# Mixer B of a hybrid Mamba/FFN kernel: a tile's diagonal products in two visits, and the second tile's other TensorE work in a new order

## What is computed

```python
proj = layernorm(x) @ in_proj_w * mup            # z (1024), xBC (1280), dt (64)
xBC = silu(causal_conv4(xBC) + conv_b)            # x, B, C
dt = softplus(dt + dt_bias);  A = -exp(A_log)
state = state * exp(dt * A) + (dt * x) outer B    # over time, here in chunks of 128 tokens
y = C . state + D * x
out = (y * rsqrt(mean(y**2) + eps)) * norm_w * silu(z)
return out @ out_proj_w
```

## Time and profile before

| | |
|---|---|
| median of 3 runs (lowest, highest) | 2864.6 us (2864.31, 2865.05) |
| span of the profiled execution | 2859.7 us |
| TensorE matmul busy | 2733.3 us, 96% |
| VectorE busy | 2009.9 us, 70% |
| ScalarE busy | 1527.0 us, 53% |
| GpSimd busy | 926.1 us, 32% |
| mean granted TensorE clock | 0.980 |

### The profile page before, as it was taken

One profiled execution on the slowest core, in us unless ns is written; L12 is line 12 of the kernel. 1 busy time (PEld: TensorE's weight loads), 2 busy tenths in 40 slices (PEclk: granted clock), 3 DMA queues, 4 the chain that ended last, 5 costly groups with the idle time before them and its releaser, 6 DMA issues. The chain is left out here.

```text
span 2859.7 us, 49906 instructions
## 1 busy us (share of the span) xinstructions
PE 2733.3 (96%) x17464; PEld 1845.0 (65%) x17464; DVE 2009.9 (70%) x3695; ACT 1527.0 (53%) x2418; POOL 926.1 (32%) x614
## 2 busy tenths in 40 slices
PE   7999999999999999996899999999999999997996
PEld 6777766777766665455666666666666666664453
DVE  5666666666666663377788888888888888885267
ACT  3444444445455442341577666766667776665242
POOL 2222223222223321232233444333333334332134
PEclk9999999999999999998999999999999999998998
DMA  4000000000000034145000000000000000022333
GB/s 125 23 23 22 22 22 22 23 28 29 22 22 22 16 121 152 45 147 204 12 23 22 22 22 16 21 22 22 15 15 22 22 22 22 15 95 89 112 118 133
DMA packets 79935, 139.59 MB, mean 49 GB/s; under 512 B 17896, under 2 KB 17896, under 8 KB 78832
## 3 DMA queue, kind: packets, MB, share of 16 engines
q1 hardware_dynamic: 70752, 125.92, 12.9%
q10 hardware_dynamic: 9104, 12.63, 1.4%
HBM read 104.98 MB, written 33.55 MB: 48 GB/s over the span
## 5 line engine op out<-in xcount | busy, mean ns | idle before, releaser
L655 PE MATMUL work<-b_xnT,shared_w 128*128 128x256 f32 x2304 | 545.8, 388 | 1.8 <-DVE b_parts L1192 1.3
L655 PE MATMUL work<-a_xnT,shared_w 128*128 128x256 f32 x2176 | 509.4, 392 | 1.3
L655 PEld LDWEIGHTS work<-b_xnT,shared_w 128*128 128x128 f32 x2304 | 426.1, 191 | 90.6 <-issue 30.1
L655 PEld LDWEIGHTS work<-a_xnT,shared_w 128*128 128x128 f32 x2176 | 419.0, 195 | 73.8 <-issue 12.3
L1232 DVE TENSOR_TENSOR b_decay<-b_decay,b_gt 128x1024 f32<-128x1024 f32 x256 | 351.7, 1395 | 119.3 <-ACT b_decay L943 115.8
L936 ACT ACTIVATE b_decay<-seg 128x1024 f32<-128x1024 f32 x256 | 248.5, 1029 | 112.0 <-PE seg L781 111.8
L943 ACT ACTIVATE b_decay<-b_decay 128x1024 f32<-128x1024 f32 x256 | 266.1, 1073 | 0.0
L1406 POOL TENSOR_TENSOR b_rhs<-b_l_side,of_head 128x1024 fp32r<-128x1024 f32 x32 | 82.0, 2563 | 552.4 <-DVE b_l_side L1201 552.4
L1441 POOL TENSOR_TENSOR a_y<-a_y,a_skip 128x1024 f32<-128x1024 f32 x32 | 90.9, 2840 | 484.1 <-DVE a_y L1221 484.1
L1111 DVE SCALAR_TENSOR_TENSOR shared_cv<-shared_pre,a_conv_w,shared_cv 128x256 f32<-128x256 f32 x432 | 189.7, 482 | 74.6 <-ACT shared_cv L880 68.9
L1111 DVE SCALAR_TENSOR_TENSOR shared_cv<-shared_pre,b_conv_w,shared_cv 128x256 f32<-128x256 f32 x480 | 232.1, 517 | 14.2 <-ACT shared_cv L880 6.3
(11 more groups left out here) (314 smaller groups left out, 4612.4 us busy)
## 6 DMA issues: line engine op xcount, KB each, us to landing
shared_x<-in_L_attn_a_x SPq DMA_DIRECT2D x16, 512.0 KB, 3.5
a_x_res<-in_L_attn_a_x SPq DMA_DIRECT2D x32, 256.0 KB, 2.6
x_mid<-a_x_res SPq DMA_DIRECT2D x32, 256.0 KB, 2.1
shared_w<-in_L_ffn_d_w SPq DMA_DIRECT2D x2, 4096.0 KB, 14.0
f_d_w<-in_L_ffn_d_w SPq DMA_DIRECT2D x2, 4096.0 KB, 14.5
f_x_res<-x_mid SPq DMA_DIRECT2D x8, 1024.0 KB, 5.9
f_bc_w<-x_mid SPq DMA_DIRECT2D x8, 1024.0 KB, 5.6
shared_x<-x_mid SPq DMA_DIRECT2D x16, 512.0 KB, 3.6
```

Source lines behind the costliest of these rows:

```text
L655: mm = nc.tensor.matmul(dst, w_in[:, k, col:col + m], xnT[:, k, :], start=(k == 0), stop=(k == KD - 1))
```

## The change

Only mixer B (NP > 1) is touched. The diagonal products of a tile are done in two visits of four slots. Unit 1 of the first tile moves ahead, between `pout` and `xnT1`. In the second tile `z1` and `z2` come right behind `rt0`, `sums` comes behind `state1`, and `out0` stands behind the last unit, ahead of the last visit. ScalarE's and VectorE's orders are rewritten to match: the multiplies of slots 4 to 7 of the second tile stand behind convolution pair (8, 9), the halo copy, the state add and the copy of the sums; the gate of the first tile comes in two halves at different places; the layer norm of the supertile after next moves from the second tile to the first.

```diff
@@ mixer_phase, the lists @@
-        if NP > 2:
-
-            fill1 = [[], [], [], ["z1"], [], ["z2"]] + [[]] * (NS - 6)
-
...
-                    + (["xnT0"] if nxt else []) + (["pout"] if prev else []) + (["xnT1"] if nxt else [])
+                    + (["xnT0"] if nxt else []) + (["pout"] if prev else [])
+                    + (["seg0.1"] if NP > 1 else []) + (["xnT1"] if nxt else [])
                     + ["ident0", "small1"])
...
+            if NP > 1:
+                def diagonal(j, half):
+                    return [f"ydiag{j}.{s}" for s in range(half * (NS // 2), (half + 1) * (NS // 2))]
+
+                def when(names):
+                    return names if nxt else []
+
+                steps += when(["dt"] + blocks[0:2]) + diagonal(0, 0)
+                steps += ["seg0.2"] + when(blocks[2:4]) + ["seg0.3"] + when(blocks[4:NB])
+                steps += state_steps(0) + diagonal(0, 1) + when(["z0a", "z0b"])
+                steps += ["rs0", "yoff1a", "yoff1b", "seg1.0", "rt0"] + when(["z1"])
+                steps += ["seg1.1"] + when(["z2"]) + ["ident1"] + diagonal(1, 0)
+                steps += ["seg1.2"] + state_steps(1) + when(["sums"]) + ["seg1.3", "out0"]
+                steps += when(["small0"]) + diagonal(1, 1)
+                return steps
@@ ScalarE's supertile (square and gate now take which halves) @@
+                    if NP > 1:
+                        slot_bound(sec, 0, 2)
                     if nxt:
                         xnT_copy(sec, 1)
+                    if NP > 1:
+                        slot_bound(sec, 0, 3)
+                        slot_exp(sec, 0, 2)
+                        slot_exp(sec, 0, 3)
+                        if nxt:
+                            softplus(sec)
+                            block_copy(sec, 0)
+                            block_copy(sec, 1)
+                        slot_bound(sec, 0, 4)
+                        slot_bound(sec, 0, 5)
+                        if nxt:
+                            block_copy(sec, 2)
+                        slot_exp(sec, 0, 4)
+                        if nxt:
+                            block_copy(sec, 3)
+                        slot_exp(sec, 0, 5)
+                        slot_bound(sec, 0, 6)
+                        if nxt:
+                            block_copy(sec, 4)
+                        slot_bound(sec, 0, 7)
+                        if nxt:
+                            block_copy(sec, 5)
+                        slot_exp(sec, 0, 6)
+                        if nxt:
+                            block_copy(sec, 6)
+                        slot_exp(sec, 0, 7)
+                        if nxt:
+                            block_copy(sec, 7)
+                            block_copy(sec, 8)
+                        square(2 * i, (0,))
+                        if nxt:
+                            block_copy(sec, 9)
+                        square(2 * i, (1,))
...
+                        for s in (0, 1):
+                            slot_bound(sec, 1, s)
+                        for s in (0, 1):
+                            slot_exp(sec, 1, s)
+                        out_rsqrt(2 * i)
+                        if nxt:
+                            z_copy(sec, "z1")
...
@@ VectorE's supertile @@
+                    if NP > 1 and sec.ln is not None:
+                        norm_stats(sec.ln)
                     small_sums(sec, 1)
                     if not prev:
                         norm_into_w_out()
+                    if NP > 1:
+                        slot_mult(sec, 0, 2)
+                        if nxt:
+                            dt_raw(sec)
+                        slot_mult(sec, 0, 3)
+                        if nxt:
+                            dt_finish(sec)
+                            conv_blocks(sec, (0, 1))
+                        gate(sec, 0, (0,))
+                        if sec.ln is not None:
+                            norm_apply(sec.ln)
+                        slot_mult(sec, 0, 4)
+                        if nxt:
+                            conv_blocks(sec, (2, 3))
+                        slot_mult(sec, 0, 5)
+                        if nxt:
+                            conv_blocks(sec, (4, 5))
+                        slot_mult(sec, 0, 6)
+                        slot_mult(sec, 0, 7)
+                        exponent_sides(2 * i + 1)
+                        state_add(sec, 0)
+                        gate(sec, 0, (1,))
+                        if nxt:
+                            conv_blocks(sec, (6, 7))
+                        square_sums(sec, "rs0")
+                        from_state(sec, 1)
+                        rms_var(sec, "rt0")
+                        slot_mult(sec, 1, 0)
+                        slot_mult(sec, 1, 1)
+                        if nxt:
+                            next_decays(sec)
+                            keep_column(sec)
+                        slot_mult(sec, 1, 2)
+                        slot_mult(sec, 1, 3)
+                        if nxt:
+                            conv_blocks(sec, (8, 9))
+                            halo(sec)
+                        state_add(sec, 1)
+                        if nxt:
+                            sums(sec)
+                        for s in (4, 5, 6, 7):
+                            slot_mult(sec, 1, s)
+                        out_scale(2 * i)
+                        out_add(sec, "out0", i, 0)
+                        if nxt:
+                            small_sums(sec, 0)
+                        gate(sec, 1)
+                        if nxt:
+                            exponent_sides(2 * sec.n)
+                        return
@@ GpSimd: norm_rsqrt now in tile_steps of the first tile @@
-                tile_steps(0, 0)
-                tile_steps(0, 1, ln=2)
+                tile_steps(0, 0, ln=2 if NP > 1 else None)
+                tile_steps(0, 1, ln=None if NP > 1 else 2)
```

35 lines of the change are left out of this document (28 added, 7 removed).

## The result

The changed kernel takes 2865.7 us (median of 20 runs, 2862.0 to 2872.8), the kernel before 2863.7 in the same comparison (20 runs): a ratio of **1.0013, 95% interval 1.0007 to 1.0019**. By the ratio it is 3.7 us slower, by the two medians 2.0; both are less than the 0.2% at which I had put the limit of a measurement. The profiled span is 2866.4 us (before 2859.7).

The account below looks back on a forecast made before the run. TensorE sets the period (78.18 of 78.63 us busy), fed by VectorE's chain. Fourteen supertiles +2.1, first +1.0, last +1.6 make +4.7 on the 2859.7 span, 2864.4; the median lies 4.9 above: 2869 us, range 2853 to 2883.

Parts of the forecast that it names:

- First tile -0.75: xT0 to the second tile's first unit: 0.70 and 0.20 saved, 0.15 lost by unit 1, so 50.85 us instead of 51.60.
- The chain to S + 15.40: Second tile, S its first unit's start: VectorE's multiplies, convolution pair, halo and state add let sums start at S + 15.40.
- Exclusion: VectorE instructions with two SBUF inputs and GpSimd's SBUF reads shut each other out, so multiply 2 works from S + 9.25.
- next_decays and keep_column follow (0.7): VectorE, second tile, from S + 7.37: these take 0.7 us unheld, so multiply 2 is issued at about S + 8.1.
- the over 2 us that I gave as a sign: Second tile on VectorE: multiply 2, held by GpSimd's decay of the state, should take over 2 us.
- TensorE's own way, 13.8 to sums and 12.53 behind: Second tile: TensorE's own work takes 13.8 us from S to sums, then 12.53 from sums through the next supertile's zza.
- Nothing for the first tile's waits, the loads and GpSimd's norm step: First tile's new waits, SyncE's later x load (about 13 us to spare) and GpSimd's power step are each priced at nothing.
- slower rival: First tile's blocks wait for ScalarE's copies: 0.75 us lost per supertile, 10.5 over fourteen, 2880 us; chance 0.2.
- Period +0.15: Per supertile, first tile -0.75 and second tile +0.90 give +0.15; +2.1 over fourteen, period 78.8 us.
- First supertile +1.0, last +1.6: First: statistics and a multiply ahead of dt, +1.0 (-1 to +3). Last: no fills, half visits stall ScalarE, +1.6 (0 to +5).
- Faster rival (the chain doesn't bind): VectorE's chain in the second tile doesn't bind: 2857 us with sharing, 2847 if it never binds; chance 0.2.
- The sharing reading: VectorE's multiply and GpSimd's decay run together instead of excluding each other: chain 0.85 us shorter, 12 over fourteen, 2857 us.

Follow-up runs that it names:

- first-tile-alone run: Against the kernel before, only each supertile's first tile has the new order, with the norm in it; second tile as before but for convolution pair (8, 9): 2846.4 us, 0.9941.
- run without the decay: Changed kernel with GpSimd's decay of the state in mixer B's second tile cut to one head, so the state is wrong: 2839.3 us (1 run).
- xw early in the kernel before: Kernel before, with GpSimd's two operations that make xw moved ahead of the sum into y1 in mixer B: 2898.2 us, 1.0119.
- second alone: Against the kernel before, only each supertile's second tile has the new order; the first tile and the norm's place stay as before: 2871.3 us, 1.0030.
- decays later: Changed kernel with next_decays and keep_column moved behind multiply 3 of the second tile on VectorE: 2865.9 us, 1.0012 to the kernel before.
- out0 early: Changed kernel with the second tile's output product moved right behind unit 2 and VectorE's order behind the halo copy changed to match: 2884.9 us, 1.0089 to the kernel before.
- the same move of xw: GpSimd's making of xw put ahead of the sum into y1 in mixer B: changed kernel 2846.1 us, 0.9936; kernel before 2898.2 us, 1.0119.

## Why the prediction was right, and where not

**The outcome** (2869 forecast, 2865.7 measured, inside the range and within what I called no change) came from the mechanism that the prediction named: packed TensorE work against VectorE's chain, one paying for the other. The first-tile-alone run and the run without the decay show both sides of it. That the sum came as close as it did is luck: of the +4.7 us forecast in mixer B +4.2 were measured, but the fourteen supertiles with all fills came out at -2.4 instead of +2.1, and the first and the last at +6.6 instead of +2.6. By the steps:

- **First tile -0.75.** Measured -1.3 (51.61 to 50.31). The visits are right: 1.88 each. Visits and breaks together save 0.93 (forecast 0.90), and unit 1's new place costs 0.07 (0.15). What I left out are the yoff groups, which wait for VectorE: they took 2.12 and 2.20 us before and 1.97 and 1.91 after, 0.4 us together. The second tile's is shorter because pair (8, 9) is no longer ahead of the copy of rs0: it's 1.91 with the first tile alone too, and the run with xw early in the kernel before shows the same place as a 1.53 us wait. The first tile's belongs to the second tile's new order (2.13 with the first tile alone, 1.98 with the second alone).
- **The chain to S + 15.40.** Measured S + 15.72. Exclusion was right, and the run without the decay prices it at 1.6 us a supertile. The step that failed is "next_decays and keep_column follow (0.7)": I asked only whether a multiply is held, and let the instruction before it go free. L1220 is held from S + 7.37 to S + 9.39, and its followers stand behind the hold. Multiply 2 starts at S + 9.64 instead of working from 9.25, and itself takes 1.21 us, not the over 2 us that I gave as a sign. The convolution pair starts 0.5 us late by my walk; the halo, at 0.15 instead of 0.4, gives half of that back. The Trainium skill (SBUF — State Buffer, Who interferes with whom) names tensor_scalar among those that can take the shared ports; the trace agrees, with 2.02 us beside 0.28 for its twin.
- **TensorE's own way, 13.8 to sums and 12.53 behind.** The second is 12.51. The first is right as work: without the decay sums stands at 14.11 with a wait of 0.34, so 13.77. The waits: 1.27 in the visit (forecast 0.6) and 0.68 ahead of sums (1.0).
- **Nothing for the first tile's waits, the loads and GpSimd's norm step.** Right: no wait ahead of L667 x48, so the slower rival did not occur.
- **Period +0.15.** Measured -0.1. Two errors of opposite sign, -0.5 in the first tile and +0.3 in the second.
- **First supertile +1.0, last +1.6.** Measured +2.4 and +4.2, the larger misses. Both signs were right, and the old order takes the last supertile's +4.2 to nothing. The first wasn't summed from its rows, and 1.45 of its +2.4 are a lower clock that the profile of another kernel with the same order there doesn't have. In the last I let out0 balance the exposed slots, and left out the clock: behind the gaps it is at its lower level for a while. How the 4.2 divide between waits and clock isn't shown.
- **Faster rival (the chain doesn't bind).** It did bind. The run without the decay shows what one link of the chain costs: 1.62 us a supertile, 23 us over fourteen, more than the 17 us that the first tile gains. The sharing reading, the other half of this rival, is out: a single multiply that meets the decay takes 2.32 us (decays later), and L1220 2.02.

The slower rival's price was never paid, but the table shows where a slower result was near: the second tile alone is 1.0030, and with out0 early the change is 1.0089.

## What to carry to other kernels

When TensorE is packed tighter, walk the engine that feeds it instruction by instruction, and lay the GpSimd operations beside it: here one overlap of 1.7 us, on an instruction that itself nobody waits for at once, took all that the packing gave. Look for which instruction is ahead of the held one and which is behind; moving the held one only changes the victim, while moving GpSimd's work into a stretch where the other engine idles removes it, and the same move of xw is worth some -20 us in one order and +34 us in another. Cost the written-out first and last passes from their own rows: with no fill work there, an order made for the loop loses several us, and the last can keep the old one. When single stages are compared between two profiles, compare their granted clocks first: here 1.45 us of one supertile and 11 us of one kernel were the clock's.
